# One core, Trainium2: a quarter of a pair's gene sums ahead of two transposes on TensorE, and a third masked piece at the head of a pair on VectorE

## The reference

```
h  = einsum('bg,egp->bep', x, weight * mask) + bias      # weight (16, 5000, 128), mask (5000, 128), h (64, 16, 128)
h += attention(layernorm(h))     # 8 heads, causal over the 16 rows of each sample; low-rank q and kv, rotary part, W_o
h += moe(layernorm(h))           # 64 experts, top 2 of a sigmoid gate, plus a shared gated layer
```

## Time and profile before

| | |
|---|---|
| median of 3 runs | 293.17 us (293.15 to 295.56) |
| the profiled execution | 292.96 us |
| its span, first to last instruction | 291.2 us |
| TensorE matmul busy | 185.6 us (64%) |
| VectorE busy | 169.5 us (58%) |
| GpSimd busy | 152.5 us (52%) |
| ScalarE busy | 80.0 us (27%) |
| mean granted TensorE clock | 0.834 of full speed |

### The profile page before, as it was taken

One profiled execution on the slowest core, in us unless ns is written; L12 is line 12 of the kernel. 1 busy time (PEld: TensorE's weight loads), 2 busy tenths in 40 slices (PEclk: granted clock), 3 DMA queues, 4 the chain that ended last, 5 costly groups with the idle time before them and its releaser, 6 DMA issues.

```text
span 291.2 us, 5498 instructions
## 1 busy us (share of the span) xinstructions
PE 185.6 (64%) x2183; PEld 153.1 (53%) x2183; DVE 169.5 (58%) x429; ACT 80.0 (27%) x205; POOL 152.5 (52%) x121
## 2 busy tenths in 40 slices
PE   0079600998987886949928944977956577768200
PEld 0068500977876685837826833755845463346200
DVE  0033326956889888897897596679680311259111
ACT  2033000022232221311211213395955420035400
POOL 3237439289888977894892732053311355710070
PEclk9999955799999997996987995588977955699955
DMA  7999999999999978689999849000211216201521
GB/s 278 201 413 391 407 428 359 406 416 420 415 414 413 416 264 362 236 306 313 220 226 197 96 131 221 2 9 11 72 36 37 74 61 189 76 20 38 146 57 34
DMA packets 32899, 64.16 MB, mean 220 GB/s; under 512 B 2890, under 2 KB 25383, under 8 KB 32423
## 3 DMA queue, kind: packets, MB, share of 16 engines
q1 hardware_dynamic: 31272, 58.43, 61.6%
q10 hardware_dynamic: 576, 3.26, 2.7%
q0 software_dynamic: 1024, 2.10, 2.5%
HBM read 55.91 MB, written 7.86 MB: 219 GB/s over the span
## 4 chain that ended last, share of the span: by engine, by line
DVE 24%; PE 22%; DMA 16%; issue 13%; POOL 11%; SPq 6%; ACT 4%; another core or an unknown queue 2%; POOLq 1%; DVEq 0%; ACTq 0%
DMA ring<-in_L_tok_weight_dram 14%; PE bank L766 5%; POOL ring L428 4%; DVE ring L1122 3%; POOL mask L470 3%; DVE bank L1177 3%; PE bank L954 3%; SPq L327 3%; DVE mask L1284 2%; PE bank L940 2%; DVE bank L1156 2%; DVE prod L1152 2%; DVE prod L1174 2%; SPq L333 2%
## 5 line engine op out<-in xcount | busy, mean ns | idle before, releaser
L428 POOL TENSOR_TENSOR ring<-ring,mask 128x896 f32<-128x896 f32 (+1 forms) x48 | 92.3, 1951 | 25.4 <-DMA ring<-in_L_tok_weight_dram 25.4
L766 PE MATMUL bank<-ring,xT 128*64 128x128 f32 x1248 | 82.4, 290 | 2.4 <-DVE ring L1122 1.2
L766 PEld LDWEIGHTS bank<-ring,xT 128*64 128x64 f32 x1248 | 74.5, 147 | 7.2 <-DVE ring L1122 3.2
L1122 DVE TENSOR_TENSOR ring<-ring,bank 128x1024 f32<-128x1024 f32 (+1 forms) x45 | 46.2, 1047 | 39.0 <-DMA ring<-in_L_tok_weight_dram 38.8
L417 POOL TENSOR_TENSOR rstd<-mv,half 128x1 f32<-128x1 f32 (+1 forms) x24 | 14.5, 607 | 34.1 <-DVE mv L1133 34.1
L502 POOL DMA_INDIRECT ring<-expert_outputs,gather_index x16 | 16.0, 1003 | 27.5 <-DMA expert_outputs<-ring 23.3
L470 POOL TENSOR_TENSOR mask<-ring,mask 128x512 f32<-128x512 f32 x8 | 10.4, 1302 | 37.9 <-ACT ring L637 37.9
L448 POOL DMA_INDIRECT expert_inputs<-xf,scatter_index x16 | 16.3, 1021 | 6.3 <-issue 3.8
L911 PE MATMUL bank<-w,ring 128*64 128x128 f32 (+1 forms) x256 | 15.2, 300 | 2.2 <-ACT ring L626 2.2
L940 PE MATMUL bank<-w2p,ring 128*128 128x128 f32 (+1 forms) x128 | 16.1, 313 | 0.6 <-ACT ring L647 0.6
L1177 DVE TENSOR_REDUCE bank<-prod 128x128 f32<-128x256 f32 (+7 forms) x8 | 16.4, 2047 | 0.0
(11 more groups left out here) (139 smaller groups left out, 306.9 us busy)
## 6 DMA issues: line engine op xcount, KB each, us to landing
ring<-in_L_tok_weight_dram SPq DMA_DIRECT2D x48, 832.0 KB, 10.4
expert_inputs<-prod ACTq DMA_DIRECT2D x3, 1024.0 KB, 14.6
ring<-expert_inputs SPq DMA_DIRECT2D x6, 512.0 KB, 6.0
expert_outputs<-ring SPq DMA_DIRECT2D x12, 256.0 KB, 2.3
mask<-in_L_tok_mask_dram SPq DMA_DIRECT2D x3, 832.0 KB, 16.6
w<-in_x_dram SPq DMA_DIRECT2D x1, 1250.0 KB, 14.1
w2p<-in_L_ffn_w_dram SPq DMA_DIRECT2D x1, 1024.0 KB
w2p<-in_L_ffn_w_dram SPq DMA_DIRECT2D x1, 768.0 KB
```

What stands on the lines that cost most here:

```text
L428: pool.tensor_tensor(unit(j, q, SPLIT(q // 2), UC), unit(j, q, SPLIT(q // 2), UC), mask[:, (m + SPLIT(q // 2)) * D:(m + UC) * D], ALU.mult ...
L766: last = pe.matmul(bank[0][64 * par:64 * par + 64, 0:D], xT[:, (UC * t + c) * B:(UC * t + c + 1) * B], unit(j, 2 * t + par, c, c + 1), sta ...
L1122: dve.tensor_tensor(both(j, t, a, b), both(j, t, a, b), m.rearrange("p (u f) -> p u f", u=1).to_broadcast([P, 2, (b - a) * D]), ALU.mult). ...
```

## The change

VectorE masks three pieces at the head of a turn, none between `scores` and `less_max`; the two pieces in between take the places one share earlier. TensorE issues `sum_genes(c, 0)` ahead of `turn_o` and `turn_xn`, and `sum_genes(c, 1)` where `sum_genes(c, 0)` stood.

```diff
-VECTOR_SHARE = (2, 1, 1, 1, 1)
+VECTOR_SHARE = (3, 1, 1, 1, 0)
...
                 project_b, attend_d = b >= 0, d >= 0
+                sum_genes(c, 0)
                 if attend_d:
                     turn_o(d)
                 if project_b:
                     turn_xn(b)
-                sum_genes(c, 0)
+                sum_genes(c, 1)
                 if attend_d:
                     attend(d)
                 if project_b:
                     project(b)
-                for n in range(1, 4):
+                for n in range(2, 4):
                     sum_genes(c, n)
                 if attend_d:
                     turn_xf(d)
```

## The result

The changed kernel took 295.0 us (median of 20 runs, 292.16 to 298.32), the kernel before 293.56 us in the same measurement (20 runs, 289.75 to 295.56). The ratio is 1.0075, with a 95% interval of 1.004 to 1.0111: slower by 0.75%, where the forecast was 0.2% faster, 292.7 us. The time lies in the forecast range, but the sign is wrong. Executions of one kernel differ by several us here, with the mean granted clock; the ratios leave the disturbed ones out.

A forecast was written before the change was run, and what follows sets the result against it. VectorE was taken to bound turns 5 to 7. Turn 1's +2.3 and turn 3's +0.8, less later gains, end the loop at -0.5: 292.5 us profiled, 292.7 as median; range 290.0 to 296.3.

The forecast's parts named there:

- What bounds the kernel: In turns 5 to 7 VectorE is the bound, TensorE counting only through its waits; in turn 4 GpSimd is the last.
- Turn 1, +2.8 on GpSimd and +2.3 on `norm_qk`: Piece (2,1h), waiting for its DMA, precedes `stats_h(0)`: GpSimd's `root_h(0)` 2.8 us later, `norm_qk(0)` 2.3 later.
- Turn 3, +0.8 for TensorE's order: Head of turn 3: `sum_genes(3, 0)` waits for the `keep_h` copy, so TensorE takes 0.8 us more up to `attend`.
- The sum for `add_attended` of turn 3, +3.1: `add_attended` of turn 3 comes 3.1 us later: 2.3 from turn 1 and 0.8 from TensorE's order.
- Heads of 3.1 us, and 3.6 us won from turn 3 on: Three pieces take 3.1 us from `o` to `add_attended`, against 3.71 in turns 6 and 7; lateness falls by 3.6 after turn 3.
- The clock: Sums moved into TensorE's wait for `o` may keep its clock up, `attend` ready at 2.3 or 2.8 us; sum unchanged.
- rival C: Turns 6 and 7: clock still low at `turn_qk`, `choose` and `place` later, 2.2 us per turn, 297.1 us; chance 0.09.
- -0.5 was forecast: At the loop's end the early delays and late gains sum to 0.5 us earlier than in the profiled execution.
- Rival D, the transfers: TensorE frees ring units 2.3 to 3.5 us later, so the weights' DMA falls behind: up to 3.5, 296.2 us; chance 0.08.

The follow-up runs named there:

- the filled kernel: The changed kernel with 2 to 5 extra identity matmuls before `turn_xf` in each of turns 2 to 7, filling TensorE's holes: 294.25 us beside 290.83 of the kernel before.
- the last experiment: Both parts of the change from turn 5 on alone, no extra matmuls, against the kernel before: 289.99 us beside 293.63, no ratio given.

## Why the prediction was wrong

- *What bounds the kernel*: right. From turn 5 on VectorE, in turn 4 GpSimd: in the changed kernel its two roots of turn 4 run back to back again, at 102.77.
- *Turn 1, +2.8 on GpSimd and +2.3 on `norm_qk`*: right. Alone it measured 3.0 and 2.5, with no later gain or loss. The limit of (3,0h) in turn 2, of the same size, was missed; in the three traces of the changed kernel this piece ended some 0.2 us after the root.
- *Turn 3, +0.8 for TensorE's order*: right, 0.96 alone. The sum for `add_attended` of turn 3, +3.1, was met within 0.6 us by the second and third trace (+2.6, +3.3) and the filled kernel (+3.7) and missed by the first (+5.3).
- *Heads of 3.1 us, and 3.6 us won from turn 3 on*: right, 3.06 to 3.07 and 3.8.
- *The clock*: the step that failed. I wrote of turn 2 that all sums "go with it", so took the 8.9 us from `turn_qk` to the end of pair 2's sums as they stood at the upper clock, and gave rival C, "the clock comes back too late", only turns 6 and 7, at 0.09. It came about in turn 2 or turn 4. In all three traces of the changed kernel the clock fell once between `turn_qk` of turn 2 and 128 us, and the loop ended at +1.44, +1.56 and +1.52; with the holes filled it did not fall there, and the loop ended at -0.30, where -0.5 was forecast. From `add_attended` of turn 4 (L1201) to the next `o` were 17.1 and 18.3 us in the two traces with the fall in that turn, 15.3 in the first and the filled one. So a fall took 1.8 and 3.0 us of that turn, and 1.7 to 1.9 us of the loop; the second figure rests on one trace of the filled kernel, whose extra matmuls cost something themselves. In turn 4 it acts as C says: `gate`, `qkv` and the rank stand between `choose` and `place`. Third trace: 10.9 us from `choose` to `o`; first, with the clock up: 9.3.
- Why there: the change takes 16 records out of the stretch between `turn_o` and `turn_qk` and makes `norm_qk` and the roots late, so the holes in front of `turn_qk` and `turn_xf` grow, from 1.07 to 1.98 us in turn 2 and from 1.05 to 0.5 + 1.7 in turn 4. The kernel before has its fall at the head of turn 5, where `gate` and `qkv` come after the clock has risen again, and pays some 0.6 us for it (2.88 us from `o` to `add_attended` and not 2.27). I priced these waits at nothing, since VectorE and not TensorE was the bound. The Trainium skill ("TensorE: Matmul & The Clock Gate", What's actually happening), that recent activity sets the clock, fits these traces (0.50 behind the longer holes in six of eight, 1.00 behind the shorter ones); I had used it for the one wait that the change shortens and not for those that it lengthens.
- *Rival D, the transfers*: no part. From 75 us on no engine waits for the weights' DMA, in any of the three traces of the changed kernel.
- What stays open: the measured ratio is 2.2 us (0.0075 x 293.56). The three traces of the changed kernel end the loop at +1.5 on average, the two of before at 0 and +0.69, so the loop explains some 1.2 us. The other 1.0 would lie behind it, where kernels with the same instructions take 113.4 to 117.6 us; no run ties that to the change. And filling the holes brought no gain in the measured time (294.25 us beside 290.83), so what the falls cost is shown in the loop's marks alone. That the longer holes bring the falls is shown by the count of turn 4 (six of eight traces, none of seven), not by a rate over many executions of one kernel: only profiled ones show where the clock fell.

## What to carry to other kernels

A wait that costs nothing on an engine that isn't the bound can still cost its clock: before work is taken out of a stretch of TensorE, look at the holes that stay there, and ask whether a half-speed `gate` or `qkv` behind them would be on the path. And a piece that waits for a transfer should not be moved ahead of a short instruction on which another engine's queue hangs: here 1.2 us of masking moved past one norm's statistics made everything behind it 2.5 us later. An order that pays in the steady turns can be given to these alone, as the last experiment does (its gain is likely, not shown).

## What the runs showed of the hardware

The same hole does not always bring the fall. In front of `turn_xf` of turn 4 two of eight traces with 1.66 or 1.67 us kept the clock. Before `turn_qk` of turn 2 the hole was 1.98 us in the first and in the third trace of the changed kernel. Behind it the first worked at 0.50, and the third (windows, 2 us each) kept 1.00:

```profile
68.00:70.00 2.00, 0.40 (x8) 0.15 (x4) 2.00 (x4) 0.00 (x0) 1.89 (x3) 1.00 1.02 419
70.00:72.00 2.00, 1.63 (x23) 1.28 (x23) 0.91 (x3) 0.80 (x2) 2.00 (x2) 1.00 1.03 426
```

The second had fallen earlier, at 64.5 us, behind a wait of 1.35 us for `keep_h`, so that its sums took up most of the hole, and was back at 1.00 at `turn_qk`. So the fall must be reckoned as a chance for each hole.

A small instruction on VectorE can be held up by one on GpSimd. VectorE's last step of `stats_qk(0)`, in the changed kernel and before:

```profile
66.61 1.26 DVE L1134 TENSOR_SCALAR mv<-mv 128x2 f32<-128x2 f32 x1
```

```profile
66.15 0.17 DVE L1133 TENSOR_SCALAR mv<-mv 128x2 f32<-128x2 f32 x1
```

1.26 us for 2 elements and not 0.17: GpSimd's third unit ran until 61.67 + 6.17 = 67.84, and the instruction ended at 67.87. Before, that unit had ended at 66.14, just ahead of it. In the second and third trace the instruction took 0.80 and 1.52 us and again ended 0.02 to 0.04 us behind the unit. Both read and write SBUF alone. The Trainium skill ("SBUF — State Buffer", Who interferes with whom) describes a port that VectorE and GpSimd share and that whoever issues first holds for a whole instruction, against a tensor_scalar among others; these rows agree. It cost little here, as `norm_qk` waited for the root that came behind the same unit: in the changed kernel the piece behind this instruction, started at 67.78, ended only some 0.2 us after the root.
